# Constants instead of counts in the waits of TensorE: a GRU and an attention GRU on one core

## The reference, cut to what matters

```python
def gru_step(h, x):                       # 1024 steps, batch 512, 64 units
    rec = h @ Wh + b_rec                  # x is keys[t] @ Wx + b_in
    z = sigmoid(xz + rz); r = sigmoid(xr + rr)
    hh = relu(xh + r * rh)
    return z * h + (1 - z) * hh           # every h is kept: outs

logit = einsum('tbu,bu->bt', outs, queries @ W_att.T)
attn = softmax(logit, axis=-1)            # over the 1024 steps

def agru_step(h, x, a):                   # 1024 steps again; x is outs[t] @ Wx + b
    rec = h @ Wh
    r = sigmoid(xr + rr)
    c = relu(xc + r * rc)
    return (1 - a) * h + a * c            # a is attn[t], one number a row
```

## Time and profile before

| what | value |
|---|---|
| median of 3 runs | 5017.2 us (5017.17 to 5021.21) |
| the profiled execution | 5020.63 us |
| its span | 5018.8 us |
| granted TensorE clock, mean | 0.997 of full speed |
| PE busy, products | 4494.5 us (90%), 131196 |
| PE busy, weight loads | 3831.3 us (76%), 131196 |
| DVE busy | 4400.3 us (88%), 24625 instructions |
| ACT busy | 2302.1 us (46%), 9363 instructions |
| POOL busy | 2719.8 us (54%), 6154 instructions |
| DMA | 108 GB/s mean, 41.4% of 16 engines in the loads and stores |

### The profile page before, as it was taken

One profiled execution on the slowest core, in us unless ns is written; L12 is line 12 of the kernel. 1 busy time (PEld: TensorE's weight loads), 2 busy tenths in 40 slices (PEclk: granted clock), 3 DMA queues, 4 the chain that ended last, 5 costly groups with the idle time before them and its releaser, 6 DMA issues.

```text
span 5018.8 us, 354200 instructions
## 1 busy us (share of the span) xinstructions
PE 4494.5 (90%) x131196; PEld 3831.3 (76%) x131196; DVE 4400.3 (88%) x24625; ACT 2302.1 (46%) x9363; POOL 2719.8 (54%) x6154
## 2 busy tenths in 40 slices
PE   7888888888888888888888799999999999999999
PEld 6777777777777777777777688888888888888887
DVE  7888888888888888888888799999999999999998
ACT  4555555555555555555555343434434344443443
POOL 5666666666666666666666344444444444444444
PEclk9999999999999999999999899999999999999999
DMA  3333333333333333333333455555555555555554
GB/s 89 101 99 95 101 98 96 101 95 99 101 95 99 101 93 101 101 93 101 99 95 105 114 125 121 121 125 119 124 122 120 124 120 124 122 121 125 119 124 110
DMA packets 169275, 544.13 MB, mean 108 GB/s; under 512 B 31644, under 2 KB 38060, under 8 KB 169260
## 3 DMA queue, kind: packets, MB, share of 16 engines
q1 hardware_dynamic: 169260, 543.93, 41.4%
HBM read 405.24 MB, written 138.56 MB: 108 GB/s over the span
## 4 chain that ended last, share of the span: by engine, by line
PE 88%; issue 9%; ACT 2%; DVE 0%; DMA 0%; ACTq 0%; SPq 0%; DVEq 0%
PE r_bank_b L527 14%; PE r_bank_a L527 14%; PE c_bank_a L527 13%; PE c_bank_b L527 13%; PE z_bank_b L533 7%; PE z_bank_a L533 6%; PE logit_bank L579 5%; PE r_bank_b L533 3%; PE r_bank_a L533 3%; PE z_bank_a L527 2%; PE z_bank_b L527 2%; PE c_bank_b L539 1%; PE c_bank_a L539 1%; ACT logit_rows L328 1%; PE c_bank_b L533 1%
## 5 line engine op out<-in xcount | busy, mean ns | idle before, releaser
L312 POOL TENSOR_TENSOR a_kept<-attn_rest,state 128x128 f32<-128x128 f32 x2048 | 935.1, 457 | 1302.9 <-DVE state L504 1267.8
L295 POOL TENSOR_TENSOR kept<-z_gate,h 128x128 f32<-128x128 f32 x2048 | 932.2, 455 | 991.7 <-ACT z_gate L339 991.7
L285 POOL TENSOR_TENSOR prod<-h,qw 128x128 f32<-128x128 f32 x2050 | 940.1, 459 | 0.0
L533 PE MATMUL r_bank_a<-x,weights 64*64 64x128 f32 x8200 | 879.9, 286 | 5.6 <-DMA bias_w<-bias_part 4.9
L533 PE MATMUL r_bank_b<-x,weights 64*64 64x128 f32 x8192 | 876.4, 285 | 0.0
L579 PE MATMUL logit_bank<-prod,row_sum 64*64 64x128 f32 x8208 | 849.6, 269 | 0.7 <-POOL prod L285 0.7
L533 PE MATMUL z_bank_a<-x,weights 64*64 64x128 f32 x8200 | 845.9, 279 | 2.0 <-issue 2.0
L533 PE MATMUL z_bank_b<-x,weights 64*64 64x128 f32 x8192 | 844.0, 279 | 0.0
L434 DVE SCALAR_TENSOR_TENSOR vec_bank<-vec_bank,z_rest 128x64 f32<-128x64 f32 x4096 | 734.3, 225 | 0.0
L445 DVE TENSOR_TENSOR h<-vec_bank,kept 128x64 f32<-128x64 f32 x4096 | 718.6, 217 | 0.1
L527 PE MATMUL r_bank_a<-h,weights 64*64 64x128 f32 x4096 | 446.4, 287 | 264.6 <-issue 183.6
(11 more groups left out here) (119 smaller groups left out, 19151.7 us busy)
## 6 DMA issues: line engine op xcount, KB each, us to landing
x<-in_keys_t SPq DMA_DIRECT2D x512, 256.0 KB, 3.7
gru_outputs<-h SPq DMA_DIRECT2D x256, 512.0 KB, 3.4
x<-gru_outputs SPq DMA_DIRECT2D x512, 256.0 KB, 3.7
attn<-attention SPq DMA_DIRECT2D x512, 256.0 KB, 4.5
logits<-logit_rows SPq DMA_DIRECT2D x258, 8.0 KB
time_rows<-logits SPq DMA_DIRECT2D x2, 896.0 KB, 6.5
attention<-time_rows SPq DMA_DIRECT2D x2, 896.0 KB, 5.5
weights<-in_weight_columns SPq DMA_DIRECT2D x2, 176.0 KB, 3.9
```

Source lines behind the costliest of these rows:

```text
L285: nc.gpsimd.tensor_tensor(prod[:, (s - 1) % BODY, gcols(g)], h_at(s - 1)[:, gcols(g)], qw[:, gcols(g)], ALU.mult).then_inc(prod_ready[g], 1)
L295: nc.gpsimd.tensor_tensor(kept[:, g], z_gate[:, g], h_at(s - 1)[:, gcols(g)], ALU.mult).then_inc(kept_ready[g], 1)
L312: nc.gpsimd.tensor_tensor(a_kept[:, s % 2, gcols(g)], attn_rest[:, s % 2, gcols(g)], state[:, (s - 1) % 2, gcols(g)], ALU.mult).then_inc(a ...
L533: last = nc.tensor.matmul(dst[lanes(half)], weights[lanes(1 - half), w], moving[lanes(1 - half)], start=start, stop=False, skip_group_chec ...
```

## The change

The loops count within a body. PE's semaphores that it waits for are brought back by 8 in every body, through an extra increment by -8 (-4 for two of them) that rides on a product issued after the last wait of that body. So the count that PE waits for is the same constant in every body: `s + 1` for what belongs to its own group, `seen_by_pe(s, o)` for what the other group's engines count, `ANEW[s - 1]` for a_new, whose semaphore is split by the parity of the step. The waits move out of instructions of their own into the products, and each stands at the product that needs it. `h_ready` alone stands at the r product, `xz_summed` at the z product, `xh_summed` at the candidate's, `prod_ready` at the logit's; `r_ready` and `cand_ready` of the other group stand at the x products that overwrite what they guard, and `xr_summed` of the other group at the second half of x's candidate product. In the attention loop `agated_ready` and `akept_ready` stay counts in registers with `alone`, and `axr_summed` moves to the kept product for r.

The increments by -8 are 16 in a GRU body and 10 in an attention body, 3328 in all. Some readers on other engines had to follow. DVE waits for constants where it reads a semaphore that PE brings back. At the first step of a body DVE now waits also for the r product (`r_summed`, `ar_summed`) and counts `bodies_begun` up with an instruction of its own, once for each group. SP's store of h waits for `z_summed` one step later in place of `h_ready` (`h_last` at the end), and its load of attention rows waits for `s_ready` in place of `anew_ready`. After the loops a few semaphores (`h_last`, `x_last`) say what the counts of 1025 said before.

```diff
+        FIRST = BODY + 1
+
+        def seen_by_pe(s, g):
+            return s + 2 if g == 0 else (s + 1 if s else FIRST)
+
+        ANEW = [s // 2 + 1 + s % 2 for s in range(BODY)]
...
             def store_outs(k, b):
                 for g in GROUPS:
-                    sp.wait_ge(h_ready[g], k * BODY + (CHUNK * (b + 1) + 1))
+                    if isinstance(k, int) and b == 1:
+                        sp.wait_ge(h_last[g], 1)
+                    else:
+                        sp.wait_ge(z_summed[g], k * BODY + (CHUNK * (b + 1) + 2))
...
                     for g in GROUPS:
-                        sp.wait_ge(anew_ready[g], k * BODY + (CHUNK * (b + 1) + 1))
+                        sp.wait_ge(s_ready[g], k * BODY + (CHUNK * (b + 1) + 1))
...
             def gru_gated(due, s, g):
+                if s == 0:
+                    dve.wait_ge(r_summed[g], due)
+                    dve.sem_inc(bodies_begun, 1)
                 dve.wait_ge(rh_summed[g], due)
-                dve.wait_ge(r_ready[g], due)
+                dve.wait_ge(r_ready[g], s + 2)
...
             def agru_gated(due, s, g):
-                dve.wait_ge(ar_ready[g], due)
+                if s == 0:
+                    dve.wait_ge(ar_summed[g], due)
+                    dve.sem_inc(bodies_begun, 1)
+                dve.wait_ge(ar_ready[g], s + 2)
...
-            def from_x(dst, w, moving, start):
+            def from_x(dst, w, moving, start, then=None):
                 for half in range(HALVES):
+                    if half == 1 and then:
+                        pe.wait_ge(*then)
...
-            def add_bias(dst, part, stop=False):
+            def add_bias(dst, part, stop=False, taken=None):
...
+                    if half == 0 and taken:
+                        last.then_inc(*taken)
...
             with pe.Fori(0, T, BODY) as t0:
-                soon, full = count(0, t0, 1), count(2, t0, BODY)
+                full, loads = count(0, t0, BODY), [count(1, t0 * PAIRS, 32), count(2, t0 * PAIRS, 64)]
                 for s in range(BODY):
-                    due, soon = soon, count((s + 1) % 2, t0, s + 2)
                     for g in GROUPS:
...
-                        alone()
-                        if next_chunk:
-                            pe.wait_ge(x_loaded[n // CHUNK % 2], loads)
+                        pe.wait_ge(h_ready[g], s + 1)
+                        own(r_bank[g][:, 0:GC], GH_R, hs, False, True).then_inc(r_summed[g], 1)
+
+                        pe.wait_ge(r_ready[o], seen_by_pe(s, o))
+                        if g == 1 and n % CHUNK == 0:
+                            pe.wait_ge(x_loaded[n // CHUNK % 2], loads[n // BODY])
+                        gru_x_r(o, n, (zr_ready[g], -BODY) if first else (h_ready[g], -BODY) if final else None,
+                                (cand_ready[g][1], -BODY) if first else None)
+
+                        pe.wait_ge(xz_summed[g], s + 1)
+                        own(z_bank[g][:, 0:GC], GH_Z, hs, False, True).then_inc(z_summed[g], 1)
+
+                        pe.wait_ge(xh_summed[g], s + 1)
+                        own(hid_part(g), GH_H, hs, False, True).then_inc(rh_summed[g], 1)
+
+                        pe.wait_ge(zr_ready[o], seen_by_pe(s, o))
+                        gru_x_z(o, n, (xz_summed[g], -BODY) if final else None, (xh_summed[g], -BODY) if final else None)
+
+                        pe.wait_ge(prod_ready[g], s + 1)
                         if s == 2 and g == 0:
                             pe.wait_ge(logits_copied, full)
-                        pe.wait_ge(prod_ready[g], due)
-                        pe.wait_ge(xr_summed[g], due)
-                        pe.wait_ge(xz_summed[g], due)
-                        pe.wait_ge(r_ready[o], due_o)
-                        pe.wait_ge(h_ready[g], due)
-                        own(r_bank[g][:, 0:GC], GH_R, hs, False, True).then_inc(r_summed[g], 1)
-                        gru_x_r(o, n)
-                        own(z_bank[g][:, 0:GC], GH_Z, hs, False, True).then_inc(z_summed[g], 1)
-
-                        alone()
-                        pe.wait_ge(zr_ready[o], due_o)
-                        pe.wait_ge(xh_summed[g], due)
-                        own(hid_part(g), GH_H, hs, False, True).then_inc(rh_summed[g], 1)
-                        gru_x_z(o, n)
                         mm = logit(i, g, i == BODY - 1)
...
-                        alone()
-                        pe.wait_ge(cand_ready[o][1], due_o)
-                        last = gru_x_h(o, n)
+                        pe.wait_ge(cand_ready[o][1], seen_by_pe(s, o))
+                        used = ((x_used, CHUNK) if g == 0 and s % CHUNK == CHUNK - 1
+                                else (r_ready[o], -BODY) if n % BODY == 0 else None)
+                        gru_x_h(o, n, (xr_summed[o], n + 1), used, (prod_ready[g], -BODY) if final else None,
+                                (xr_summed[o], -BODY) if final else None)
...
+                        pe.wait_ge(anew_ready[g][(s - 1) % 2], ANEW[s - 1])
+                        own(r_bank[g][:, 0:GC], AH_R, ns, False, True).then_inc(ar_summed[g], 1)
+
+                        pe.wait_ge(ar_ready[o], seen_by_pe(s, o))
...
                         alone()
-                        pe.wait_ge(axr_summed[o], due_o)
                         pe.wait_ge(agated_ready[o], due_o)
                         pe.wait_ge(akept_ready[o], due_o)
-                        own(hid_part(o), AH_C, from_kept(o, n), True, False)
-                        own(r_bank[o][:, 0:GC], AH_R, from_kept(o, n), False, False)
+                        last = own(hid_part(o), AH_C, from_kept(o, n), True, False)
...
+                        pe.wait_ge(axr_summed[o], n + 1)
+                        last = own(r_bank[o][:, 0:GC], AH_R, from_kept(o, n), False, False)
...
-                        alone()
-                        pe.wait_ge(acand_ready[o], due_o)
-                        last = agru_x_c(o, n)
+                        pe.wait_ge(acand_ready[o], seen_by_pe(s, o))
+                        agru_x_c(o, n, (x_used, CHUNK) if g == 0 and s % CHUNK == CHUNK - 1 else None,
+                                 (axr_summed[o], -BODY) if final else None)
```

More of the change, by code:

```diff
@@ L241, in _ @@
             sp.wait_ge(x_used, T)
-            sp.wait_ge(xh_summed[0], T + 1)
+            sp.wait_ge(x_last, 1)
             for b in range(2):
@@ L317, in _ @@
             for g in GROUPS:
-                for q in (r_ready[g], z_ready[g], zr_ready[g], ar_ready[g]):
-                    act.sem_inc(q, 1)
+                act.sem_inc(z_ready[g], 1)
+                act.sem_inc(zr_ready[g], FIRST)
+                for q in (r_ready[g], ar_ready[g]):
+                    act.sem_inc(q, (1, FIRST)[g])
             act.sem_inc(rest_ready, 1)
@@ L588, in _ @@
             gru_x_h(0, 0)
+            pe.wait_ge(xr_summed[0], 1)
+            for g in GROUPS:
+                for q in (r_ready[g], ar_ready[g]):
+                    pe.wait_ge(q, (1, FIRST)[g])
+                for q in (zr_ready[g], cand_ready[g][1], acand_ready[g]):
+                    pe.wait_ge(q, FIRST)
+                pe.wait_ge(anew_ready[g][1], BODY // 2 + 1)
+            pe.wait_ge(anew_ready[1][0], BODY // 2)
             with pe.Fori(0, T, BODY) as t0:
-                soon, full = count(0, t0, 1), count(2, t0, BODY)
+                full, loads = count(0, t0, BODY), [count(1, t0 * PAIRS, 32), count(2, t0 * PAIRS, 64)]
@@ new lines, in _ @@
+                        first, final = s == 0, s == BODY - 1
+                        pe.wait_ge(h_ready[g], s + 1)
[5 more added lines that the diff above has]
+                                (cand_ready[g][1], -BODY) if first else None)
@@ L623, in _ @@
                             mm.then_inc(logits_summed, 1)
-                        alone()
-                        pe.wait_ge(cand_ready[o][1], due_o)
-                        last = gru_x_h(o, n)
-                        if g == 0 and s % CHUNK == CHUNK - 1:
-                            last.then_inc(x_used, CHUNK)
+                        pe.wait_ge(cand_ready[o][1], seen_by_pe(s, o))
[3 more added lines that the diff above has]
+                                (xr_summed[o], -BODY) if final else None)
+            pe.wait_ge(xh_summed[0], 1)
+            pe.sem_inc(x_last, 1)
+            for g in GROUPS:
+                pe.wait_ge(h_ready[g], 1)
+                pe.sem_inc(h_last[g], 1)
             for i in (BODY - 2, BODY - 1):
                 for g in GROUPS:
-                    pe.wait_ge(prod_ready[g], T + i - (BODY - 3))
+                    pe.wait_ge(prod_ready[g], i - (BODY - 3))
                     mm = logit(i, g, i == BODY - 1)
@@ L687, in _ @@
                 soon = count(0, t0, 1)
+                loads = [count(2, t0 * PAIRS, 32 * (BODIES + 1)), count(3, t0 * PAIRS, 32 * (BODIES + 3))]
                 for s in range(BODY):
@@ L692, in _ @@
                         o, n, due_o = 1 - g, s + g, (due, soon)[g]
```

(24 more changed lines are left out.)

77 lines of the change are left out of this document (44 added, 33 removed).

## The result

The changed kernel takes 4430.17 us (median of 4 runs, 4428.79 to 4430.53) against 5017.18 us, a ratio of 0.8828 (95% interval 0.8813 to 0.8844): 587 us less. The prediction was 4490 us with a range of 4370 to 4675, and 527 us less. The profiled execution took 4430.53 us, its span is 4428.7 us.

A forecast was written before the change was run, and what follows sets the result against it. PE was taken to bound the kernel, closing its loops by waits for its own sums. Gains of 366 us (GRU) and 161 (attention) sum to 527, taking 5020.6 to 4494, put at 4490 us; range 4370 to 4675.

The forecast's parts named there:

- PE closed the GRU loop on itself through xz_summed: GRU loop, PE ahead of r: waiting for PE's own sum, then three waits and the load, makes a turn 1.32 us.
- A wait inside a product costs 0.05 us: PE's products: 0.05 us from the end of h or a_new to the load; 0.27 for PE's own sums.
- Rival A: Recurrence answers late: a wait in a product costs 0.20 us after h and a_new; 4579 us, chance 0.14.
- DVE becomes the bound of the GRU loop: GRU loop: DVE's queue needs 2.23 us a step, 1.115 a turn, covering PE's 0.98; body 18.68, gain 366 us.
- The body's start: First turns of a GRU body: 0.30 on DVE, 0.09 first turn, 0.3 bodies_begun, 0.15 logits wait and loop's end.
- the logits' move: GRU loop: wait for copied logits moves behind r, z and candidate products; with the loop's end, 0.44 us becomes 0.15.
- The attention loop: Recurrence 1.83 us a step, DVE's queue 1.88 and so the bound; body 15.92, gain 161 us.
- B: Attention loop keeps its turn: axr_summed at r's kept product holds PE, body stays 17.18; 4651 us, chance 0.12.
- C: Increments on PE's products cost half a slot, 0.055 us each, 183 us for 3328; 4673 us, chance 0.02.
- the sum by the Trainium skill's rule: The 3328 increments on PE's products serialise at about 26 ns each, 88 us, making the forecast 4578.
- D: No change: a wait for PE's own sum passes only when PE's queue runs empty; 5017 us, chance 0.03.
- E: Slower: loads whose product waits can't be drawn ahead, 0.13 us each; near 6640 us, chance 0.07.

The follow-up runs named there:

- e2: Kernel before, with only the xz_summed wait moved from ahead of r to ahead of z, still a register wait in its own instruction: 4681.3 us.
- e3: Changed kernel, with the wait for xz_summed put back at the r product, against its constant: 4474.5 us.
- f2: Changed kernel, with DVE's step-count register instructions moved in both the attention and GRU loops: 4328.9 us.
- e6: Changed kernel, with the wait and increment of bodies_begun issued twice at each place: 4462.9 us.
- e7: Changed kernel, with the wait for the copied logits put back ahead of the r product: 4515.2 us.
- f1: Changed kernel, with DVE's step-count register instruction in the attention loop moved ahead of the wait for ar_ready: 4346.3 us.
- e1: Changed kernel, with the waits for h and a_new ahead of r in an instruction of their own again, same constants: 4541.9 us.
- e4: Changed kernel, with the attention loop's wait for axr_summed put back ahead of the candidate's kept product: 4544.4 us.
- e9: Kernel before, with three waits (xz_summed, copied logits, axr_summed) moved to the products needing them, all register waits in their own instructions: 4606.0 us.
- e5: Changed kernel, with 10240 increments or decrements of a spare semaphore added on PE's products: 4444.8 us.
- e8: Kernel with both DVE register instructions moved, with CHUNK doubled to 8 for bodies of 16 steps: 6083.7 us.

## Why the prediction was right, point by point

The mechanism was right in the GRU loop and half right in the attention loop, and the sum was helped by two misses of opposite sign: the GRU loop gave 91 us more than forecast (0.71 x 128), the attention loop 35 less (0.27 x 128).

- **PE closed the GRU loop on itself through xz_summed.** Right. e2 opens it by one moved line. That three waiting instructions belong to this loop was in the sum of a turn too; e3, where one is left of the three, shows that the place alone does not close it.
- **A wait inside a product costs 0.05 us.** Right: 53 ns after h and after a_new. Rival A (0.20) fell. Even the old form costs only 115 ns, so this rival was mis-sized as well: 0.062 over the other, not 0.15.
- **DVE becomes the bound of the GRU loop.** Right, shown by f2. The step was 2.23 in the forecast and is 2.156. The term that was off is the distance ahead of group a's gated, taken as 0.22 between the bounds 0.13 and 0.52: it is 0.157. That is 0.063 x 8 = 0.50 of the 0.71 us by which the body was over-estimated.
- **The body's start.** In the GRU 0.30 + 0.09 + 0.3 + 0.15 = 0.84 was forecast, 0.72 is there; bodies_begun is the part that was too dear (e6), and I took 0.29 for the logits' move, where e7 gives 0.67.
- **The attention loop.** The recurrence was put at 1.83 and the bound at DVE's 1.88; the step is 1.963, bound by group a's recurrence. The step of the prediction that failed is "r 4008.29 to gated 4009.05 is 0.76", taken over as it stood: from r's product it is 0.88 now (4008.475 to 4009.355). Of this 0.087 is the wait for ar_ready in the register instruction (f1). For the rest, 0.03, no run was made; in the trace r's product takes 0.167 from its first record to its last where it took 0.145, and the sigmoid follows that at 0.317 where it followed at 0.307. In e1 the second is back at 0.306 and the first is not, so the last 0.01 goes with the wait inside the product. The prediction costed DVE's waits that turned into constants at nothing, without asking where they would land. At the body's start I forecast 0.88 and 0.49 is there (16.19 less 8 x 1.963), which hid more than half of the miss.
- **B** (the attention loop keeps its turn) fell. e4 and e9 show what it would have taken: the old place, or the old form.
- **C** (increments cost a slot) fell by e5, and so did the sum by the Trainium skill's rule (TensorE: Matmul & The Clock Gate, The cost: per-tile semaphore tail), 4578 us.
- **D and E** fell with the result. PE is 99% busy, and a load whose product waits is still drawn ahead: the kept product's load for r, which holds the wait for axr_summed, starts 0.11 before its product (median).

What stays open: what each of DVE's instructions at a body's start is worth, of which only bodies_begun was varied; and 0.02 of the 0.03 in the attention recurrence.

## What to carry to other kernels

Look for a wait of an engine for its own result, and for what stands between it and the next work: asked at the first product that needs it, and not one earlier, it gave 336 of 587 us here, from one line. When a wait changes its kind, look again at what instruction it ends up in on every engine that shares the semaphore: a wait that slid into a register instruction took back 84 us that no one had planned to spend. And before you unroll a loop to save its edges, see in the trace that its body still stays on the core.

## What the runs showed of the hardware that was not expected

- An increment on the product just ahead of one whose signal is awaited delays that signal by 25 ns (317 to 342), while the products keep their distance (e5).
- On PE a wait in an instruction of its own costs 0.062 us over the same wait in the product (115 against 53 ns from the end of DVE's operation to the weight load; 115 for a constant in e1 and for a register in e2), a good deal less than the 0.1 at which such instructions follow each other.
- On DVE a register instruction with the wait in it puts 0.12 us between the sigmoid and the operation, against 0.03 in the kernel before and 0.04 in f1, where the register instruction stands ahead of the wait.
- A loop body of 16 steps made PE's branch take 5.88 us instead of 0.21 (e8).
